# Reordering the work of a group in both attentions of a two-layer kernel: scores in runs of even length

## What is computed

```python
# layer 0: q, k, v of 16 heads; two softmaxes over the same values
std_out = out_proj(softmax(where(mask, scores, neg)))
gsa_scores = scores + position_sensitivity * splat_attn
gsa_out = out_proj(softmax(where(mask, gsa_scores, neg)))
return (1.0 - blend) * std_out + blend * gsa_out
# layer 1: one softmax
scores = einsum('bqhd,bkhd->bhqk', q, k) * scale
probs = softmax(where(causal, scores, min))
out = einsum('bhqk,bkhd->bqhd', probs, v).reshape(b, s, H) @ o_w
```

## Time and profile before

| | |
|---|---|
| median of 3 runs | 1895.13 us (1890.72 to 1898.94) |
| the profiled execution | 1889.23 us |
| its span, first to last instruction | 1887.4 us |
| TensorE (PE) busy | 1669.1 us, 88% of the span |
| VectorE (DVE) busy | 1469.5 us, 78% |
| ScalarE (ACT) busy | 1234.6 us, 65% |
| GpSimd (POOL) busy | 699.6 us, 37% |
| mean granted TensorE clock | 0.926 of full speed |

### The profile page before, as it was taken

How to read it: one execution, slowest core, us unless ns; L and a number is a source line. 1 busy time by engine, 2 the same in 40 slices (tenths; PEclk the granted TensorE clock), 3 DMA queues, 4 the chain that set the end, 5 groups by cost and what they waited for, 6 DMA issues and landing times. The chain is left out here.

```text
span 1887.4 us, 31938 instructions
## 1 busy us (share of the span) xinstructions
PE 1669.1 (88%) x10554; PEld 1156.6 (61%) x10554; DVE 1469.5 (78%) x3080; ACT 1234.6 (65%) x2769; POOL 699.6 (37%) x1326
## 2 busy tenths in 40 slices
PE   4959899999999888788889997888886899997999
PEld 3537544444444577577768886677764455545888
DVE  7767789999997268999997969999446789826655
ACT  3633477888777534788986768888652588865322
POOL 2001222222222215666675646666232111224632
PEclk9979799999999899888889999989987799988999
DMA  3464143233330100000000000000038223110000
GB/s 123 140 217 68 35 75 86 52 59 69 69 69 2 45 1 1 1 1 1 1 1 1 1 1 1 1 1 1 1 105 191 44 54 67 36 58 18 13 12 23
DMA packets 36996, 82.27 MB, mean 44 GB/s; under 512 B 9952, under 2 KB 12384, under 8 KB 35936
## 3 DMA queue, kind: packets, MB, share of 16 engines
q1 hardware_dynamic: 36192, 78.65, 17.0%
q10 hardware_dynamic: 640, 1.57, 0.4%
HBM read 52.53 MB, written 27.26 MB: 42 GB/s over the span
## 5 line engine op out<-in xcount | busy, mean ns | idle before, releaser
L1167 ACT ACTIVATE probs<-pss 128x512 f32<-128x512 f32 (+3 forms) x1152 | 481.6, 495 | 129.0 <-PE pss L1130 127.9
L873 DVE TENSOR_REDUCE negmax<-px 128x2 f32<-128x1024 f32 (+2 forms) x480 | 508.5, 1113 | 45.0 <-PE px L855 42.1
L1730 POOL TENSOR_SCALAR rp<-sw,tau 128x256 f32<-128x256 f32 x720 | 343.0, 512 | 7.1
L1234 POOL TENSOR_SCALAR_AFFINE_SELECT probs<-probs 128x512 f32<-128x512 f32 x192 | 120.8, 637 | 506.1 <-ACT probs L1167 506.1
L1130 PE MATMUL pss<-queries,keys 64*128 64x512 f32 (+3 forms) x1152 | 295.9, 396 | 5.6 <-ACT probs L1167 4.3
L855 PE MATMUL px<-keys,queries 63*128 63x512 f32 (+3 forms) x1152 | 266.3, 418 | 10.5 <-DVE negmax L873 10.5
L1130 PEld LDWEIGHTS pss<-queries,keys 64*128 64x128 f32 x1152 | 167.5, 191 | 152.5 <-ACT probs L1167 134.7
L1144 PE MATMUL po<-probs,vals 128*32 128x512 f32 (+3 forms) x2304 | 248.7, 508 | 0.4 <-POOL probs L1234 0.2
L1585 PE MATMUL pss<-again,sw 128*128 128x256 f32 x1024 | 248.9, 402 | 0.0
L1887 DVE BATCH_NORM_STATS2 st<-rp 128x6 f32<-128x512 f32 x360 | 229.6, 675 | 0.9 <-POOL rp L1730 0.9
L1585 PEld LDWEIGHTS pss<-again,sw 128*128 128x128 f32 x1024 | 206.6, 206 | 29.9
(11 more groups left out here) (375 smaller groups left out, 2548.1 us busy)
## 6 DMA issues: line engine op xcount, KB each, us to landing
queries<-rec_q SPq DMA_DIRECT2D x92, 128.0 KB, 3.6
keys<-rec_k SPq DMA_DIRECT2D x92, 128.0 KB, 3.6
queries<-rec_q SPq DMA_DIRECT2D x92, 64.0 KB, 3.4
keys<-rec_k SPq DMA_DIRECT2D x92, 64.0 KB, 3.4
rec_q<-fs SPq DMA_DIRECT2D x16, 256.0 KB, 4.2
rec_k<-fs SPq DMA_DIRECT2D x16, 256.0 KB, 4.4
rec_q<-vals SPq DMA_DIRECT2D x16, 256.0 KB, 3.0
rec_k<-vals SPq DMA_DIRECT2D x16, 256.0 KB, 3.6
```

The source lines that it names most:

```text
L873: return e.tensor_reduce(out, from_px, X_AXIS, ALU.max, negate=True)
L1167: e.activation(tl.probs[arg][:, w, :], tl.pss[scores % 3][:, 512 - width:512], ACT.Exp).then_inc(self.exp_made, 1)
L1730: x = e.tensor_scalar(self.rp[rp % 6][:, :, h], self.view(g, q)[:, h, :], -BIG, self.tau[r][:, 2 * q + h:2 * q + h + 1], ALU.min, ALU.max)
```

## The change

The two strings in `ORDERS` are replaced, and nothing else. Both have the same letters as before: 48 `s`, 20 `m`, 12 `v`, 2 `d`, 2 `t` and one `r`. The scores stand in runs of two or four where they stood in runs of one, two or three. The other letters are moved by at most one score, so that an even number of scores stands ahead of each of them: the `d`s from 17 and 31 scores to 18 and 30 with two kinds, the second `d` from 27 to 28 and the first `t` from 19 to 20 with one kind (the first `d` stays at 16), the `t`s from 43 to 44 with two kinds. The `r` stays at 40 and 42.

```diff
-    ORDERS = {1: "mmsssvmssmsvmsssmvsmsssmsssdmssstsmssmvmsssmvsmsvvdssmsmvsssmvmsssmvssmsvsssrtsssvsss", 2: "mmssvmsmssvmssmsvsmsssmsmsssvsmdsssmvsmssmvsmssvsmsvsmssdmsmssvmsssmvsssvrsssttsssvss"}
+    ORDERS = {1: "mmssssvmmssvmssmssvmssmssssdmsssstmssmvmssmssvmssvvdssmmvssmssvmssmvssmssvssrtssssvss", 2: "mmssvmssmssvmssmvssmssmssmssvssmdssmvssmmssvmssvmssvssmdssmmssvmssmssvssvrssssttssvss"}
```

## The result

The changed kernel takes 1977.2 us (median; 1965.9 to 1982.0) against 1895.1 before: ratio 1.0438, 95% interval 1.0413 to 1.0464, so 82 us slower. Forecast were 1947 us, 52 more, and a range up to 1972, so the measured time lies above the range. The direction was right, the size was not.

What follows compares the result with a forecast made beforehand. TensorE was taken to set the pace in issue order, partly through waits on score and maxima tiles. Added waits of 34.8 + 19.7 = 54.5 us on 1895.1 gave 1949.6, taken as 1947 us; 8-in-10 range 1892 to 1972.

Steps and rivals of the forecast that it cites:

- the ring of three score tiles: Score buffers `pss`, both attentions: the fourth score of a run starts no earlier than 1.09 us after the first.
- The rule that matmuls start and end strictly in program order: TensorE's array halves: the forecast counted each half in its own order; under this rule pairing gives 1870.6 us, chance 0.05.
- The drain's part: First attention, fifth segment: 1.40 to 1.99 us, as the values step waits for a drain moved behind a late score.
- the sum of 54.5 us: Both attentions: 15 x 2.32 + 7 x 2.81 us a group, 34.8 + 19.7 = 54.5 us slower.
- the price of a late score: Segments with four scores: a plain run ends 1.09 + 0.32 = 1.4 us after its start.
- the last group: Each attention: first and last groups count half, lacking values steps or maxima, giving 15 and 7 effective groups.
- the clock as a rival: Steady part: gaps on TensorE lower its granted clock, streams take 10% more, 40 us, 1987 us; chance 0.06.
- The range: Whole kernel: 8 in 10 for 1892 to 1972 us; 1.3 times the lengthening gives 1947 + 22 = 1969.
- The first step of the prediction: Both attentions: TensorE sets the 25.9 us group period, partly through waits on two rings, score tiles and maxima tiles.
- Signs that were named: Changed profile: periods near 28.2 and 28.7 us, score-load waits well above 61 us, ScalarE and VectorE about 73 and 84% busy.
- Rival 1: Both attentions: fourth scores' waits cost nothing, only saved slots count; 1877.5 us (chance 0.09) or 1870.6 (0.05).
- Rival 2: Both attentions: only about a third of the lengthening appears, cancelling the savings; 1886 to 1905 us, chance 0.10.

## Why the prediction was right in direction and too low in size

**What held.** The direction, and the ring of three score tiles as the reason for the loss. The fourth score started 1.09 and 1.07 us after the first, as priced. Without that wait at least 68 of the 82 us are gone, with two tiles the two orders change places, and the exchange of products confirms that the halves run each in its own order. The rule that matmuls start and end strictly in program order (the Trainium skill, page "TensorE: Matmul & The Clock Gate", section "Part 3: Packing small matmuls"), which was weighed in the prediction, does not hold between the halves; here the measurement decides. The drain's part, named in the prediction for the fifth segment, is most of what was left of a steady group of the first attention.

**The step that failed: the sum of 54.5 us, in two of its terms.** The attentions grew by 84.0 us. The 29.5 between are 16.4 in the steady groups, 11.2 in the last groups, and 1.9 in the first groups and the period before the last of the second attention.

**The term that was mis-sized: the price of a late score.** The prediction let a values step follow a late score after 0.32 us, the time after a pair that was on time. It is 0.43 at 512 columns (1626.88 to 1627.31) and 0.36 at 384. Measured lengths of the first attention's segments, in the order of the prediction's list: 1.00, 1.61, 0.86, 2.49, 2.16, 1.61, 0.67, 0.67, 3.28, 1.79, 0.37, 1.27, 0.31, 0.26. Ten of fourteen are longer than carried, six of them by 0.06 to 0.10, two by 0.17 and 0.20, and one is shorter. In sum a group is 3.12 us above before instead of 2.32, in the second attention 3.84 instead of 2.81. Over the 14 full periods of the first and the 5 of the second that is 14 x 0.80 + 5 x 1.03 = 16.4 us. The main cause is the load in the open, and not only at late scores: the pairs that follow a values step, carried at 0.29 and 0.25, took 0.37 and 0.31. With the short loads these segments come down to about what was carried, 0.29 and 0.23, and so do others, 3.20 for the carried 3.21 and 1.71 for 1.70. In the second attention a part is left: its fifth segment took 1.35, with short loads too, for the carried 1.09, and no run shows why.

**The term that was missing: the last group.** It was counted at half a group's excess, 1.2 and 1.4 us. Measured are 39.6 against 30.5 and 33.6 against 29.0, 9.2 and 4.6 more: 11.2 us beyond the sum. The prediction had the clock as a rival only for the steady part, where it stayed at 1.00 in the profile. It fell where no maxima keep TensorE busy between the waits. That it is the clock is shown by the added products for the first attention: 39.6 to 31.7. For the second it is less clear, 33.6 to 32.7. And the rival for the steady part was not empty: in the trace of the new string in the second attention alone, one steady group took 32.4 us instead of 29.7, at a granted clock of 0.89, and in that of the moved drain three were longer by 1.2 to 2.7 us. The clock stayed at 1.00 in every steady group of the old order with three tiles, in every trace.

**The range.** Its upper end took 22 us for a lengthening 1.3 times as large. By the prediction's own sums it is 0.3 x (15 x 3.31 + 7 x 4.44) = 24, and the step from 1949.6 down to 1947, for roundings upward, had no measured ground: what was carried came out too short.

**The first step of the prediction.** It said that TensorE sets the pace, and that part of that pace is made by the ring of score tiles. In the old order that part was nothing: taking the waits for exponentials out gained no time, since TensorE streamed through them (2.1 us idle of 300). TensorE sets the pace in some segments alone. The segments of 2.33 and 2.82 us, for instance, hold 2560 and 3072 columns, which is 1.15 and 1.38 us at 0.45 ns; in them the maxima wait for the reductions two back. That VectorE's chain bounds these is read from the traces; no run made the reductions shorter.

**Signs that were named.** The periods rose, as said, to 29.0 and 29.75 rather than 28.2 and 28.7. Busy shares of 73 and 84% for ScalarE and VectorE were 72 and 81. The loads' wait for exponentials, forecast "well above" 61 us, was 67.2: a bad sign to name, since it counted many waits in the kernel before that cost nothing. The waits that grew in proportion are those of the engines behind: VectorE for products, from 6.7 to 24.5, and ScalarE for scores, from 58.6 to 84.6.

**Rival 1,** the pairing wins, named the condition that the waits cost nothing. They could be made nearly so, and the new order was still 14 us behind, 5 with the drain put back. The saved slots did appear: in the changed kernel the four segments of the first attention that lost a slot are 0.17, 0.22, 0.22 and 0.12 us shorter, 0.73 a group where 0.63 was counted. Even with the waits taken out the other segments lengthened by more. Rival 2 (a third of the lengthening) did not occur.

## What to carry to other kernels

Set the length of a burst on an in-order engine against the number of buffers that it fills before the first comes back: with three, the fourth waits a whole round trip, 1.09 us here, and one slot saved is 0.22. Which waits in a profile cost something is not told by their sum: the loads' waits of 61.4 us hid behind matmuls that stood idle for 2.1. Look at the idle time of the engine itself, and at whose chain runs without a pause through the stretch. And price the last pass of a loop by itself, since the work that is missing there can cost the clock.

## What the runs showed of the hardware

- The wait for a tile stands at the load of weights, so a late matmul finds its load not yet made. At 384 columns the next step over all rows came 0.36 us after it instead of 0.26, and 0.29 with a load of 32 columns in place of 128.
- The two halves of the array, used by products of 63 or 64 rows, run independently enough that the exchange of two products in each of 20 places of a group moved its period by under 0.02 us.
- A last group whose matmuls stood idle four times, for 0.26 to 0.84 us, ran at 0.55 to 0.69 of the clock for 21 us, though TensorE was shown busy 83 to 98% of that time. With 40 more products it ran at 1.00, shown busy 89 to 93%.
